# First roots and squares moved to GpSimd, first products issued by operand, 24 filler matmuls: a two-layer MLP kernel on one core

## The chip, the cores and the metric

One Trainium2 chip, one core. The time is device microseconds (us) of one execution. Engines are named as in the profile: PE (TensorE), DVE (VectorE), ACT (ScalarE), POOL (GpSimd), SP (SyncE, which issues most DMAs).

## The reference

x is (2, 2048, 512). Layer 0 is a conditioned RMS norm, a gated MLP and an 8-bit/ternary down projection; layer 1 is an adapter whose weights are themselves made from the condition.

```python
scale = cond @ norm_w.T + 1.0
ms = mean(x * x, axis=-1)
h = x * (scale * rsqrt(ms + 1e-6))
val, gate = split(h @ up_w.T)              # up_w: 4096 x 512
h = val * gelu(gate)
y = act_quant(h) @ weight_quant(down_w).T + x
Wd_b = Wd + 0.1 * (cond @ Wdd.T + bdd)     # Wdd, Wdu: 65536 x 128
Wu_b = Wu + 0.1 * (cond @ Wdu.T + bdu)
out = y + relu(y @ Wd_b.T + bd) @ Wu_b.T + bu
```

## The kernel before, in words

Rows of x are taken in eight blocks of 512 tokens, two blocks (0 and 1, then 2 and 3, and so on) to a stage. In each stage 16 quads (`for n in range(NQ)`) compute the up projection of two blocks with seven products p1 to p7 per quad (a Strassen-like scheme: `product(n, p)`, lines 1351 to 1355), each product of two operands split into a high and a low fp16 part. `t_mov` holds the moving operands made of x, `u_e` and `u_l` the rows of `up_w`. In between run the adapter weights (`adapter_group(g)`, line 1406, 32 x 512 f32 matmuls on the tiles loaded from `Wdd` and `Wdu`), the down projection and, late, the adapter itself.

Every engine has its own program, written out by hand; each runs strictly in its written order, and semaphores (`wait_ge`) tie them together. The change touches the prologue, the first 40 us:

- ACT squares blocks 0 and 1 (`first_squares`, line 972), DVE adds the squares (lines 1791 and 1798), PE multiplies the sums with a tile of ones (`stat(0)`, line 1420, for block 0, `stat1(0)` and `stat1(1)`, line 1429, for block 1), and DVE makes the mean (`mean_square`, line 1822) and ten small chained instructions of inverse square root (`rsqrt(0)`, `rsqrt(1)`, lines 1834 to 1850).
- PE spreads the roots over the partitions (`spread_rs(0)` into `b_ps`, `spread_rs(1)` into `c_ps`, line 1439). DVE then scales x by them: `x_scaled(0, ...)` in two halves for block 0 and `x_scaled(1)`, four instructions, for block 1 (line 1876).
- ACT (`t_high`, line 1058) and DVE (`t_low`, line 1907) split the scaled x into the moving operands B11, B21, B12, B22. PE runs `first_product` for each (lines 1383, 1389, 1393).
- On PE the order around it is: first product of B11, `adapter_group(0)`, `spread_rs(1)`, `adapter_group(1)` and `(2)`, first product of B21, `adapter_group(3)`, `bounds(1, 2)`, `adapter_group(4)`, the products of B12 and B22, `adapter_group(5)` and `(6)`, and then quad 1.
- POOL sets `ones` and `ident` (lines 872 to 875), waits for both roots (`s_rs` 2) and then runs `weight_sums` (lines 898 to 905), sums of rows of `up_w` which ACT and DVE split from quad 1 on. At the end of each stage POOL runs `partition_all_reduce` (lines 916, 927, 934), and in stage 1 also `down_sums` (line 949), elementwise sums.

POOL's program also holds instructions called MODIFY_POOL_CONFIG in the trace and ISA in the instruction order; the build puts one ahead of the first elementwise instruction behind a `partition_all_reduce`, and one ahead of the first `partition_all_reduce` behind an elementwise one.

## Time and profile before

| | us |
|---|---|
| median of 3 runs | 839.31 |
| the three runs | 839.36, 838.85, 839.31 |
| the profiled execution | 840.44 |
| its span, first to last instruction | 838.7 |
| PE busy | 821.2 |
| DVE busy | 664.3 |
| ACT busy | 399.8 |
| POOL busy | 121.3 |

The profiled execution's own time lies 1.7 us over its span (launch and end around it) and 1.1 us over the median of the runs. A timeline row gives the start and the length of an instruction (or of a merged few), and in brackets the idle time of its engine ahead of it and what ended that. The clock column PEclk prints 1.00 in all stretches of this profile.

### The profile page before, as it was taken

To read this page: it belongs to the slowest core of one execution; us is meant where nothing else is said; L and a number is where in the kernel's file an instruction comes from. 1 tells how busy PE (TensorE), PEld (TensorE's weight loads), DVE (VectorE), ACT (ScalarE), POOL (GpSimd) and SP (SyncE) were. 2 spreads that over 40 slices of the span, in tenths; PEclk is the share of its full clock that TensorE was granted. 3 is DMA by queue.
4 is the path that set the end of the run, shared out by engine and by line. 5 is a ranking of instruction groups with operands and counts; after the bars stand their busy time and mean duration, and the time that the engine had idled before them with its cause. 6 is when DMAs were issued, how large, how long until landed. Compare 5 with 4: busy or idle time off the path is not lost.

```text
span 838.7 us, 11856 instructions
## 1 busy us (share of the span) xinstructions
PE 821.2 (98%) x3914; PEld 359.4 (43%) x3914; DVE 664.3 (79%) x968; ACT 399.8 (48%) x653; POOL 121.3 (14%) x91
## 2 busy tenths in 40 slices
PE   5999999999999999999999999999999999999998
PEld 4334444444344334444444444444444444444443
DVE  5998787889878889767787678988986586675986
ACT  5778887776454532227445543326433333324000
POOL 0363332302001153300101011100200000001000
PEclk9999999999999999999999999999999999999999
DMA  9879989666899862377798865337247435435232
GB/s 343 338 257 347 343 289 297 233 217 226 303 347 366 330 218 95 136 271 272 280 326 303 304 223 191 116 95 255 72 137 239 138 95 189 138 95 176 101 125 76
DMA packets 64860, 186.65 MB, mean 223 GB/s; under 512 B 7072, under 2 KB 8352, under 8 KB 64416
## 3 DMA queue, kind: packets, MB, share of 16 engines
q1 hardware_dynamic: 64512, 185.63, 63.5%
q8 instruction: 33, 0.54, 0.3%
q10 hardware_dynamic: 288, 0.26, 0.1%
q14 instruction: 27, 0.22, 0.1%
HBM read 154.41 MB, written 30.41 MB: 220 GB/s over the span
## 4 chain that ended last, share of the span: by engine, by line
PE 85%; DVE 5%; issue 3%; ACT 1%; DVEq 0%; ACTq 0%
PE b_ps L1351 9%; PE b_ps L1355 9%; PE b_ps L1353 9%; PE aux_ps L1406 6%; PE a_ps L1351 6%; PE aux_ps L1464 6%; PE a_ps L1355 6%; PE a_ps L1353 6%; PE c_ps L1351 3%; PE aux_ps L1542 3%; PE e_ps L1351 3%; PE e_ps L1355 3%; PE e_ps L1353 3%; PE c_ps L1353 3%; PE c_ps L1355 3%
## 5 line engine op out<-in xcount | busy, mean ns | idle before, releaser
L1954 DVE SCALAR_TENSOR_TENSOR h_ring<-v_sb,unscale,gelu 128x512 f32<-128x512 f32 x63 | 55.5, 881 | 58.0 <-ACT gelu L1092 31.9
L1351 PE MATMUL b_ps<-t_mov,u_l 128*128 128x512 f16 x252 | 95.5, 379 | 3.8 <-DVE c_ps L1915 3.6
L1355 PE MATMUL b_ps<-t_mov,u_l 128*128 128x512 f16 x252 | 95.5, 379 | 0.0
L1353 PE MATMUL b_ps<-t_mov,u_l 128*128 128x512 f16 x252 | 95.5, 379 | 0.0
L1978 DVE TENSOR_TENSOR hmax<-gelu,hmax 128x512 f32<-128x512 f32 x120 | 88.6, 740 | 7.8 <-ACT gelu L1098 2.9
L1068 ACT ACTIVATE b_ps<-a_ps 128x512 f32<-128x512 f32 x63 | 36.7, 582 | 94.1 <-PE a_ps L1355 93.9
L1102 ACT ACTIVATE gelu<-h_ring 128x512 f32<-128x512 f32 x64 | 40.3, 629 | 67.6 <-DVE h_ring L1954 67.6
L2013 DVE TENSOR_TENSOR h_ring<-h_ring,qscale 128x1024 f16<-128x1024 f32 x48 | 64.7, 1387 | 0.0
L1084 ACT ACTIVATE gelu<-a_ps,unscale 128x512 f32<-128x512 f32 x64 | 43.7, 682 | 43.3 <-DVE hmax L1978 41.1
L916 POOL PARTITION_ALL_REDUCE yscale<-hmax x8 | 17.9, 2266 | 321.0 <-DVE hmax L1978 320.3
L1098 ACT ACTIVATE gelu<-h_ring 128x512 f32<-128x512 f32 x64 | 40.2, 628 | 45.6 <-DVE h_ring L1964 45.3
L1964 DVE SCALAR_TENSOR_TENSOR h_ring<-b_ps,unscale,gelu 128x512 f32<-128x512 f32 x64 | 47.8, 747 | 15.9 <-PE b_ps L1355 15.5
L1092 ACT ACTIVATE gelu<-c_ps,unscale 128x512 f32<-128x512 f32 x64 | 43.9, 686 | 32.9 <-PE c_ps L1355 32.9
L1406 PE MATMUL aux_ps<-w_ring,cond_sb 128*32 128x512 f32 x480 | 58.1, 599 | 0.0
L1075 ACT ACTIVATE p_sb<-e_ps 128x512 f32<-128x512 f32 x63 | 37.5, 595 | 37.5 <-PE e_ps L1355 27.4
L1923 DVE TENSOR_TENSOR v_sb<-b_ps,p_sb 128x512 f32<-128x512 f32 x63 | 43.3, 687 | 11.4 <-PE b_ps L1355 11.2
L1351 PE MATMUL e_ps<-t_mov,u_e 128*128 128x512 f16 x126 | 47.8, 379 | 0.8 <-DVE u_e L1743 0.8
L1351 PE MATMUL b_ps<-t_mov,u_e 128*128 128x512 f16 x126 | 47.8, 379 | 0.8 <-ACT b_ps L1068 0.8
L1351 PE MATMUL a_ps<-t_mov,u_e 128*128 128x512 f16 x126 | 48.0, 381 | 0.0
L1351 PE MATMUL c_ps<-t_mov,u_l 128*128 128x512 f16 x126 | 47.8, 379 | 0.1
L1353 PE MATMUL e_ps<-t_mov,u_e 128*128 128x512 f16 x126 | 47.8, 379 | 0.0
L1355 PE MATMUL e_ps<-t_mov,u_e 128*128 128x512 f16 x126 | 47.8, 379 | 0.0
(264 smaller groups left out, 1701.4 us busy)
## 6 DMA issues: line engine op xcount, KB each, us to landing
w_ring<-in_Wdu SPq DMA_DIRECT2D x64, 512.0 KB, 6.0
w_ring<-in_Wdd SPq DMA_DIRECT2D x56, 512.0 KB, 7.2
u_l<-ul_dram SPq DMA_DIRECT2D x48, 512.0 KB, 4.7
u_e<-ue_dram SPq DMA_DIRECT2D x48, 384.0 KB, 3.2
h_ring<-in_up_w SPq DMA_DIRECT2D x16, 512.0 KB, 6.4
x_sb<-in_x SPq DMA_DIRECT2D x8, 1024.0 KB, 7.9
res<-in_down_w SPq DMA_DIRECT2D x16, 512.0 KB, 7.1
ul_dram<-u_l SPq DMA_DIRECT2D x15, 512.0 KB, 5.6
```

What stands on the lines that cost most here:

```text
L1084: act.activation(gelu1[:, :], a_ps[n % 2][:, :], ACT.Gelu, scale=unscale[:, s // 2, j:j + 1]).then_inc(s_g1, 1)
L1092: act.activation(gelu2[:, :], c_ps[:, :], ACT.Gelu, scale=unscale[:, s // 2, j:j + 1]).then_inc(s_g2, 1)
L1351: pe.matmul(ps[:, :], weight(n, p, 0, k), hi, start=fresh and k == 0, stop=False, skip_group_check=True)
L1353: pe.matmul(ps[:, :], weight(n, p, 0, k), lo, start=False, stop=False, skip_group_check=True)
L1355: mm = pe.matmul(ps[:, :], weight(n, p, 1, k), hi, start=False, stop=k == 1, skip_group_check=True)
L1406: mm = pe.matmul(ps[32 * q:32 * q + 32, :], cond_sb[:, :], w_tile(n)[:, 512 * (q % 2):512 * (q % 2) + 512], start=True, stop=True)
L1464: mm = pe.matmul(ps[:, :], w, q_slot(d, at + c)[:, TB * t:TB * t + TB], start=fresh and c == 0, stop=c == HC - 1, skip_group_check=True)
L1923: dve.tensor_tensor(v_sb[:, :], b_ps[n % 2][:, :], p5_sb[:, :], ALU.add)\
L1954: dve.scalar_tensor_tensor(out=h_slot(n)[:, TB:TS], in0=val[:, :], scalar=unscale[:, s // 2, j:j + 1], in1=gelu2[:, :], op0=ALU.mult, op1= ...
L1964: dve.scalar_tensor_tensor(out=h_slot(n)[:, 0:TB], in0=b_ps[n % 2][:, :], scalar=unscale[:, s // 2, j:j + 1], in1=gelu1[:, :], op0=ALU.mul ...
L1978: dve.tensor_tensor(total, absolute, total, ALU.max).then_inc(done, 1)
L2013: dve.tensor_tensor(q_slot(s, c), h_slot(NP * s + c), qscale[:, :], ALU.mult)\
```

## The change

- POOL sets a third tile, `power` (-0.5), and computes the two inverse roots itself: `first_roots(t)` raises the mean squares to that power with one 128x4 elementwise instruction each. DVE's `rsqrt(0)` and `rsqrt(1)` go; the later `rsqrt` calls stay.
- The squares of block 1 are summed to one tile by DVE (a third addition, `second_sum_squares(2)`), then over the partitions by a `partition_all_reduce` on POOL, between the two `first_roots`. DVE masks the result with `ident` and reduces it. PE's `stat1(0)` and `stat1(1)` go, and so does the wait for them ahead of SP's loads of the tiles 8 to 11 of `Wdd` (the squares now lie elsewhere in `h_ring`).
- PE runs 16 matmuls on the tile of ones (read as fp16, 256 columns, into `a_ps1`, whose contents are not used) ahead of its first work and 8 more behind it.
- PE's two first products (B11) are written out operand by operand: the terms that need only high parts first, those that need low parts behind them.
- ACT makes B21's high part ahead of `row_sums(2)` and waits for `s_rs` 2 ahead of `stage_group(1)`.

```diff
@@ -295,6 +295,7 @@
         ms_half = sb("ms_half", [P, 2 * NT])
+        power = sb("power", [P, NT])
         rs = sb("rs", [P, 2, 2 * NT])
@@ -313,6 +314,10 @@
         aux_ps = [ctx.enter_context(nc.psum_tensor(f"aux_ps{n}", [P, TB], F32)) for n in range(2)]
+        first_squares1 = [h_ring[:, k, TB:TS] for k in range(KD)]
+        first_total = h_ring[:, 2, TB:TS]
+        first_grid = first_total.rearrange("p (t q) -> p t q", t=NT)

@@ -605,8 +610,6 @@
                 if n in EARLY_SLOT:
-                    if n >= 8:
-                        sp.wait_ge(s_stat1, 2)
                     sp.dma_start(w_tile(n), src[n]).then_inc(s_w_early[n], 16)
@@ -871,7 +874,8 @@
             pool.memset(ident[:, :], 1.0).then_inc(s_const, 1)
-            pool.wait_ge(s_const, 2)
+            pool.memset(power[:, :], -0.5).then_inc(s_const, 1)
+            pool.wait_ge(s_const, 3)
             pool.affine_select(out=ident[:, :], in_=ident[:, :], compare_op=ALU.is_equal, fill=0.0,
@@ -918,7 +922,18 @@

-            pool.wait_ge(s_rs, 2)
+            def first_roots(t):
+                pool.wait_ge(s_ms, t + 1)
+                cols = slice(NT * t, NT * t + NT)
+                pool.tensor_tensor(rs[:, 0, cols], ms[:, cols], power[:, :], ALU.pow)\
+                    .then_inc(s_rs, 1)
+            first_roots(0)
+            pool.wait_ge(s_sq1, 3)
+            pool.partition_all_reduce(first_total, first_squares1[0], P, AR.add)\
+                .then_inc(s_stat1, 1)
+            first_roots(1)
             for j in SUM_ORDER:
@@ -969,7 +984,8 @@
                     act.wait_ge(s_x0[KD * t + k], 16)
-                    act.activation(h_ring[:, KD * t + k, 0:TB], x_sb[:, t, k, :], ACT.Square)\
+                    act.activation(h_ring[:, k, TB * t:TB * t + TB], x_sb[:, t, k, :],
+                                   ACT.Square)\
                         .then_inc(s_sq, 1)
@@ -1193,9 +1209,10 @@
             u_high(0, 2)
+            t_high(0, B21)
             row_sums(2)
             stage_group(0)
-            t_high(0, B21)
+            act.wait_ge(s_rs, 2)
             stage_group(1)
@@ -1356,12 +1373,7 @@

-            def first_product(ps, first_half, val, m):
-                if first_half and val:
-                    pe.wait_ge(s_first_hi, 1)
-                else:
-                    pe.wait_ge(s_uhi, part_count(0, 0 if first_half else 2))
+            def first_operands(first_half, val, m):

@@ -1373,13 +1385,17 @@

-                if m == B11:
-                    pe.wait_ge(s_first_row, 1)
+                return rows, split
+            def first_product(ps, first_half, val, m):
+                rows, split = first_operands(first_half, val, m)
+                if first_half and val:
+                    pe.wait_ge(s_first_hi, 1)
                 else:
-                    pe.wait_ge(s_thi, split_count(0, m))
+                    pe.wait_ge(s_uhi, part_count(0, 0 if first_half else 2))
+                pe.wait_ge(s_thi, split_count(0, m))
                 for k in range(2):
-                    if m == B11 and k == 1:
-                        pe.wait_ge(s_thi, 1)
                     pe.matmul(ps[:, :], rows(0, k), split(0, k), start=first_half and k == 0,
@@ -1420,16 +1436,6 @@
                 mm.then_inc(s_stat if i else s_aux, 1)
-            def stat1(part):
-                pe.wait_ge(s_sq1, part + 1)
-                row = KD + 2 * part
-                for t in range(NT):
-                    mm = pe.matmul(e_ps[:, NT * part + t:NT * part + t + 1],
-                                   h_ring[:, row, P * t:P * t + P], ones[:, 0:1],
-                                   start=True, stop=True)
-                mm.then_inc(s_stat1, 1)

@@ -1568,21 +1574,56 @@

+            half_ones = ones[:, :].bitcast(F16)
+            def keep_busy(count):
+                pe.wait_ge(s_const, 1)
+                for _ in range(count):
+                    pe.matmul(a_ps[1][:, 0:2 * P], half_ones[:, 0:P], half_ones[:, :],
+                              start=True, stop=True)
+            keep_busy(16)
             pe.wait_ge(s_small, 32)
...
             mm.then_inc(s_aux, 1)
-            pe.wait_ge(s_const, 1)
+            keep_busy(8)
             stat(0)
-            stat1(0)
             first_bounds()
-            pe.wait_ge(s_const, 3)
+            pe.wait_ge(s_const, 4)
             spread_rs(0)
-            stat1(1)
-            first_product(a_ps[0], True, False, B11).then_inc(s_p[1], 1)
-            first_product(b_ps[0], True, True, B11).then_inc(s_p[5], 1)
+            gate, val = first_operands(True, False, B11), first_operands(True, True, B11)
+            pe.wait_ge(s_uhi, part_count(0, 0))
+            pe.wait_ge(s_first_row, 1)
+            for k in range(2):
+                if k:
+                    pe.wait_ge(s_thi, 1)
+                pe.matmul(a_ps[0][:, :], gate[0](0, k), gate[1](0, k), start=(k == 0),
+                          stop=False, skip_group_check=True)
+            pe.wait_ge(s_first_hi, 1)
+            for k in range(2):
+                pe.matmul(b_ps[0][:, :], val[0](0, k), val[1](0, k), start=(k == 0),
+                          stop=False, skip_group_check=True)
+            pe.wait_ge(s_ulo, part_count(0, 0))
+            for k in range(2):
+                pe.matmul(a_ps[0][:, :], gate[0](1, k), gate[1](0, k), start=False,
+                          stop=False, skip_group_check=True)
+            pe.wait_ge(s_tlo, split_count(0, B11))
+            for k in range(2):
+                mm = pe.matmul(a_ps[0][:, :], gate[0](0, k), gate[1](1, k), start=False,
+                               stop=(k == 1), skip_group_check=True)
+            mm.then_inc(s_p[1], 1)
+            for k in range(2):
+                pe.matmul(b_ps[0][:, :], val[0](0, k), val[1](1, k), start=False,
+                          stop=False, skip_group_check=True)
+            pe.wait_ge(s_first_lo, 1)
+            for k in range(2):
+                mm = pe.matmul(b_ps[0][:, :], val[0](1, k), val[1](0, k), start=False,
+                               stop=(k == 1), skip_group_check=True)
+            mm.then_inc(s_p[5], 1)
             adapter_group(0)
@@ -1590,7 +1631,6 @@
             adapter_group(3)
-            pe.wait_ge(s_ms, 2)
             bounds(1, 2, e_ps).then_inc(s_total, 1)
@@ -1793,20 +1833,23 @@

-                row = KD + 2 * part
-                dve.wait_ge(s_sq, row + 2)
-                dve.tensor_tensor(h_ring[:, row, 0:TB], h_ring[:, row, 0:TB],
-                                  h_ring[:, row + 1, 0:TB], ALU.add).then_inc(s_sq1, 1)
+                if part < 2:
+                    dve.wait_ge(s_sq, KD + 2 * part + 2)
+                    a, b = first_squares1[2 * part:2 * part + 2]
+                else:
+                    dve.wait_ge(s_sq1, 2)
+                    a, b = first_squares1[0], first_squares1[2]
+                dve.tensor_tensor(a, a, b, ALU.add).then_inc(s_sq1, 1)

...

-                    dve.wait_ge(s_stat1, 2)
+                    dve.wait_ge(s_stat1, 1)
+                    dve.wait_ge(s_const, 4)
                     total = ms_half[:, col:col + NT]
-                    link(dve.tensor_reduce(
-                        total, e_ps[:, 0:2 * NT].rearrange("p (k t) -> p t k", k=2),
-                        AX_X, ALU.add))
+                    link(dve.tensor_tensor(first_grid, first_grid, diagonal, ALU.mult))
+                    link(dve.tensor_reduce(total, first_grid, AX_X, ALU.add))
                 elif i >= 4:
@@ -1822,15 +1865,11 @@

-            def rsqrt(i, count=1):
-                s, t = divmod(i, 2)
-                cols = slice(NT * t, NT * t + NT * count)
-                dve.wait_ge(s_ms, i + count)
-                if i == 0:
-                    dve.wait_ge(s_table, 1)
-                a, half, t = ms[:, cols], ms_half[:, cols], rs_t[:, cols]
-                y = rs[:, s % 2, cols]
+            def rsqrt(i):
+                dve.wait_ge(s_ms, i + 2)
+                a, half, t = ms[:, :], ms_half[:, :], rs_t[:, :]
+                y = rs[:, (i // 2) % 2, :]
                 link(dve.tensor_scalar(half, a, -0.5, None, ALU.mult))
@@ -2170,20 +2209,20 @@
             mean_square(0)
-            rsqrt(0)
             aux_ready(dve, "total", 0)
...
             u_low(0, 0)
+            second_sum_squares(2)
             t_low(0, B11)
...
             second_scales()
-            mean_square(1)
-            rsqrt(1)
             x_scaled(0, (2, 3))
             u_low(0, 2)
+            dve.wait_ge(s_table, 1)
+            mean_square(1)
             t_low(0, B21)
```

The order of POOL's instructions from its first tile on, before:

```order
L872 MEMSET ones 128x128
L873 MEMSET ident 128x128
L875 ISA
L875 AFFINE_SELECT ident<-ident 128x128 [waits s_const]
L898 TENSOR_TENSOR yscale<-h_ring 128x256 [waits s_u1,s_rs]
L901 TENSOR_TENSOR yscale<-yscale,h_ring 128x256 [waits s_us]
```

and now (the ISA at L934 with operands is the `partition_all_reduce`):

```order
L875 MEMSET ones 128x128
L876 MEMSET ident 128x128
L877 MEMSET power 128x4
L879 ISA
L879 AFFINE_SELECT ident<-ident 128x128 [waits s_const]
L929 TENSOR_TENSOR rs<-ms,power 128x4 [waits s_ms]
L934 ISA
L934 ISA h_ring<-h_ring 128x512 [waits s_sq1]
L929 ISA
L929 TENSOR_TENSOR rs<-ms,power 128x4 [waits s_ms]
L902 TENSOR_TENSOR yscale<-h_ring 128x256 [waits s_u1]
```

Between the affine select and the weight sums stand now two roots, one `partition_all_reduce` and two more configuration instructions, one ahead of the reduction and one ahead of the second root.

PE's order from the last matmul of the first products on, as it is now (before, the same instructions follow in the same order; the adapter group is L1406 there and the spread L1439):

```order
L1624 MATMUL b_ps<-t_mov,v_sb 128x512
L1422 MATMUL aux_ps<-w_ring,cond_sb 32x512 [waits s_w0,s_ms]
L1422 MATMUL aux_ps<-w_ring,cond_sb 32x512
L1422 MATMUL aux_ps<-w_ring,cond_sb 32x512 [waits s_w1]
L1422 MATMUL aux_ps<-w_ring,cond_sb 32x512
L1445 MATMUL c_ps<-ident,rs 128x128 [waits s_rs]
L1445 MATMUL c_ps<-ident,rs 128x128 x3
L1422 MATMUL aux_ps<-w_ring,cond_sb 32x512 [waits s_w2,s_top]
```

The spread of block 1's roots (into `c_ps`) keeps its place; all of PE's later work stands behind its wait for `s_rs`.

## Rows read from the trace of the kernel before

**Rows 1.** The page, part 1: busy us, share of the span, instructions of each engine.
```profile
PE 821.2 (98%) x3914; PEld 359.4 (43%) x3914; DVE 664.3 (79%) x968; ACT 399.8 (48%) x653; POOL 121.3 (14%) x91
```
**Rows 2.** Waits of PE, whole span: us in total, times, longest us.
```profile
PE aux_ps L1574 <- DMA cond_sb<-in_cond: 5.3, 1, 5.3
PE b_ps L1351 <- DVE c_ps L1915: 3.6, 6, 1.6
PE aux_ps L1420 <- DVE h_ring L1791: 2.5, 1, 2.5
PE e_ps L1351 <- DVE u_e L1743: 0.8, 1, 0.8
PE b_ps L1351 <- ACT b_ps L1068: 0.8, 1, 0.8
```
**Rows 3.** Busy us by stretch, 26 to 56 us; then clock, DMA share, GB/s.
```profile
26.00:36.00 10.00, 9.99 (x58) 3.83 (x62) 9.82 (x17) 6.97 (x10) 4.32 (x5) 1.00 1.03 408
...
46.00:56.00 10.00, 9.38 (x47) 3.73 (x46) 10.00 (x12) 6.99 (x12) 9.84 (x10) 1.00 0.97 342
```
**Rows 4.** Timeline of PE: start us, us, engine, line, operands.
```profile
13.90 1.09 PE L1439 MATMUL b_ps<-ident,rs 128*128 128x128 f32 x4
...
17.47 0.59 PE L1383 MATMUL a_ps<-t_mov,u_e 128*128 128x512 f16 x1
...
19.99 0.47 PE L1383 MATMUL b_ps<-t_mov,v_sb 128*128 128x512 f16 x1
20.29 0.38 PE L1389 MATMUL b_ps<-t_mov,v_sb 128*128 128x512 f16 x1
20.51 0.38 PE L1383 MATMUL b_ps<-t_mov,v_sb 128*128 128x512 f16 x1
...
22.46 0.65 PE L1439 MATMUL c_ps<-ident,rs 128*128 128x128 f32 x4
```
**Rows 5.** Timeline of DVE, prologue.
```profile
11.52 0.16 DVE L1822 TENSOR_SCALAR ms<-aux_ps 128x4 f32<-128x4 f32 x1 [0.69 <-PE aux_ps L1420]
...
13.51 0.16 DVE L1850 SCALAR_TENSOR_TENSOR rs<-rs_t,rs 128x4 f32<-128x4 f32 x1
...
15.61 1.40 DVE L1876 SCALAR_TENSOR_TENSOR x_sb<-b_ps,cs_x,x_sb 128x512 f32<-128x512 f32 x2
...
21.94 0.16 DVE L1850 SCALAR_TENSOR_TENSOR rs<-rs_t,rs 128x4 f32<-128x4 f32 x1
...
25.88 2.71 DVE L1876 SCALAR_TENSOR_TENSOR x_sb<-c_ps,cs_x,x_sb 128x512 f32<-128x512 f32 x4
```
**Rows 6.** Timeline of POOL, prologue and stage 1.
```profile
11.54 0.28 POOL L875 TENSOR_SCALAR_AFFINE_SELECT ident<-ident 128x128 f32<-128x128 f32 x1 [10.41 <-issue]
22.19 0.73 POOL L898 TENSOR_TENSOR yscale<-h_ring 128x256 f32<-128x256 f32 x1 [10.37 <-DVE rs L1850]
...
291.45 4.14 POOL L927 PARTITION_ALL_REDUCE res<-res  x1 [28.94 <-DVE res L1899]
305.85 3.82 POOL L949 TENSOR_TENSOR w_ring<-wq 128x2048 fp8e4<-128x2048 fp8e4 x1 [10.27 <-issue]
...
324.01 3.25 POOL L934 PARTITION_ALL_REDUCE res<-res  x1 [5.86 <-issue]
335.14 3.82 POOL L949 TENSOR_TENSOR w_ring<-wq 128x2048 fp8e4<-128x2048 fp8e4 x1 [7.89 <-issue]
```
**Rows 7.** The configuration instructions of line L949: ns min/median/max, first and last start.
```profile
L949 POOLq MODIFY_POOL_CONFIG  x4: 88/93/98, 295.5 to 327.2; - x4
```
**Rows 8.** Stretches as in rows 3, around POOL's gaps and in the prologue.
```profile
295.60:305.80 10.20, 10.20 (x56) 4.08 (x55) 8.01 (x13) 4.64 (x8) 0.00 (x0) 1.00 0.61 212
318.20:324.00 5.80, 5.80 (x29) 2.61 (x27) 5.32 (x17) 2.55 (x4) 0.00 (x0) 1.00 0.00 0
12.00:22.00 10.00, 9.25 (x42) 5.83 (x42) 8.46 (x35) 6.04 (x11) 0.00 (x0) 1.00 1.03 413
```
**Rows 9.** Timeline of ACT, its first use of a weight sum.
```profile
37.06 0.71 ACT L1022 ACTIVATE u_e<-yscale,um_mul 128x512 f16<-128x512 f32 x1
```

More of the change, by code:

```diff
@@ L1850, in rsqrt @@
                 dve.scalar_tensor_tensor(out=y, in0=t, scalar=1.5 * 1.5, in1=y,
-                                         op0=ALU.add, op1=ALU.mult).then_inc(s_rs, count)
+                                         op0=ALU.add, op1=ALU.mult).then_inc(s_rs, 2)
             def spread_roots(i):
@@ L2318, in _ @@
                 if j == ROOTS and s + 1 < NSB:
-                    rsqrt(2 * s + 2, 2)
+                    rsqrt(2 * s + 2)
                     if s:
```

## The prediction

> **What bounds the kernel now.** I read the page first, then the waits of PE, then the stretches and timelines of the first 60 us, POOL's timeline last. PE is busy 821.2 of 838.7 us [rows 1], so the kernel is PE's work plus 17.5 us in which PE stands. The waits show where [rows 2]: 5.3 us until the condition has landed, 2.5 us for the sum of squares of block 0, and then small ones: six waits for DVE's `c_ps` (3.6 us in all) and 0.8 us each for `u_e` and `b_ps`. Without the first two, 9.7 us of standing are left in the whole rest of the run. The stretches show the second bound: from 26 to 36 us DVE is busy 9.82 of 10 us, from 46 to 56 us all 10.00 [rows 3]. So from the moment DVE starts `x_scaled(1)` at 25.88 us [rows 5] until about 55 us DVE and PE are both nearly full, and whatever delays that start, or PE's place beside it, has nothing to hide behind. What the change adds has to be looked for on the path to that point, which is: mean of block 1, root, spread, `x_scaled(1)`.
>
> **Parts off that path.** The 24 filler matmuls have 256 columns. A 512-column matmul comes every 0.43 us at 17.47 us and every 0.22 us at 20.29 us [rows 4], while the profile grants the full clock throughout; those two rates are what 1.2 and 2.4 GHz give. So a filler costs at most 0.22 us: 16 of them 3.4 us from about 1.0 us on, inside the 5.3 us wait; 8 of them at most 1.7 us, inside the 2.5 us wait [rows 2]. Cost nothing; without that cover it would be up to 5 us. What they may bring is the higher rate earlier: the six matmuls from 17.47 to 19.99 us would take 1.3 instead of 2.5 us. Issuing the first products by operand and dropping the two groups of `stat1` also bring PE to its next task earlier. That task is `spread_rs(1)` behind one adapter group, and it waits for the root; all of this gain goes into that wait. The same goes for block 0: the root leaves DVE at 13.67 us [rows 5] and PE starts the spread at 13.90 us [rows 4]; now POOL can start it when its affine select is over, 11.54 + 0.28 = 11.8 us [rows 6], so x of block 0 is scaled some 1.3 us earlier, and DVE reaches its wait for block 1 earlier. Nothing of it survives if block 1's root is late. SP's four loads of `Wdd` tiles lose a wait that had been satisfied when the queue came to them, since they stand behind a store that starts at the same time: nothing. ACT's new wait for `s_rs` 2 holds back `stage_group(1)` and, through it, adapter group 3 on PE; both belong behind `spread_rs(1)` in any case: nothing beyond the delay itself. POOL's weight sums start after the second root instead of at 22.19 us; the first is read by ACT at 37.06 us [rows 9], 14.9 us later, and that reader moves with the delay: nothing.
>
> **The path itself: POOL.** The order shows two new configuration instructions, one ahead of the reduction and one ahead of the second root. What they cost is in POOL's timeline [rows 6]: the first elementwise instruction stands 10.41 us behind the memsets and waits for nothing shown. In stage 1 an elementwise sum stands 10.27 us behind a reduction and another, of which the order shows no wait at all, 7.89 us; the configuration instruction itself takes 0.1 us and is issued at 295.5 us, as the reduction ends [rows 7]. In the other direction a reduction stands 5.86 us behind a sum (a second such gap is 5.93 us). The gaps come with little and with much DMA traffic: 10.27 us at a DMA share of 0.61, 5.86 us at 0.00; in the prologue the share is 1.03 [rows 8]. These are switches of code, and none of them is hidden for an in-order engine.
>
> Step by step, in us from the span's start:
> - POOL free at 11.9 (11.8 and one more small memset); the mean of block 0 is there at 11.68 [rows 5]. A root of 128x4 elements on POOL has no row. It lies between 0.1 (memsets of one column) and 0.73 (a sum of 128x256 [rows 6]); I take 0.2, as it is near the small end in elements. End 12.1.
> - Switch to the reduction: 5.9, from the only rows of that direction; the upper bound is the 10.41 of the start, which had the DMA traffic. End 18.0. The third sum of squares on DVE is ready by then: it is 0.7 us of work behind `x_scaled(0)`, which before ended at 17.0 [rows 5].
> - Reduction of 128x512: 4.14 or 3.25 [rows 6]; I take 4.1, the row that also sums squares. End 22.1. DVE's mask, reduce and mean behind it (0.7 + 0.7 + 0.2, the 0.7 from the scaling instructions of the same 128x512 [rows 5]) end near 23.7, in the shadow of the next step.
> - Switch back: 10.3, between ends of 7.9 and 10.4; two of three rows say 10.3, and they are the ones with more DMA traffic. End 32.4, root 0.2, signal 0.1: PE starts `spread_rs(1)` at 32.7. Before, at 22.46 [rows 4].
>
> That is 10.2 us later for PE. By then PE has stood for about 12 us and I expect it to begin at the lower rate, as it did at 17.47 us: spread 1.1 us like block 0's [rows 4], and 1.3 us lost until the rate rises. Against that stand the small waits it will now find satisfied, 0.8 + 0.8 for `u_e` and `b_ps` [rows 2]. PE: 10.2 + 1.3 - 1.6 = 9.9. DVE starts `x_scaled(1)` at 32.7 + 1.1 + 0.1 = 33.9 instead of 25.9: 8.0 later. The two lanes then wait for each other (DVE's `c_ps` needs p6, PE's p7 needs `c_ps`), so the end moves by something between 8.0 and 9.9; I take 9.0. The stages behind follow with the same work and waits.
>
> The Trainium skill bears on the second switch ("GPSIMD Engine Reference", section 2.1): the first call into freshly loaded code pays about 6 us (5.95) that no profile row shows. The trace agrees for the switch to the reduction (5.86), not for the way back (7.89 and 10.27).
>
> **Sum.** 839.3 + 9.0 = 848.3 for the median; for a profiled execution 840.4 + 9.0 = 849.4, span near 847.7. The forecast's own ends: low, with the reduction at 3.25, the way back at 7.9, the roots at 0.1 and the end moving with DVE alone, the spread starts at 12.0 + 5.9 + 3.2 + 7.9 + 0.2 = 29.2, DVE moves by 4.5: 843.8. High, with the first switch at 10.3 under full DMA traffic and roots of 0.7: spread at 37.6, PE moves by 15.1 + 1.3 - 1.6 = 14.8: 854.1.
>
> **Rivals.**
> - *The switches are not paid here* (faster). Place: the two configuration instructions on POOL. If code of both kinds stays usable, the reduction starts with the third sum of squares, near 16.9 (x of block 0 scaled at 15.7, a 128x256 split and the sum behind it), and ends at 21.0; DVE's mean follows at 22.6, the root at 22.9, and DVE, which has one split of 1.4 us left to do ahead of it, starts `x_scaled(1)` at about 24.2, 1.7 us earlier: 837.6. The sign turns where the way back costs some 3 us, the reduction ending at 22.1: the root would then be there at 25.3, the start at 26.1. Against it: both kinds of code had been loaded before 318 us, and every change of kind still shows its gap [rows 6]. Chance 0.08.
> - *Both switches cost 6 us.* Spread at 12.1 + 5.9 + 4.1 + 5.9 + 0.3 = 28.3; PE moves by 5.8 + 1.3 - 1.6 = 5.5: 844.8. Against it is only the direction of the two gaps of 7.89 and 10.27 us. The skill's figure for the first call (same page and section) gives the same case. Chance 0.10.
> - *The delay is absorbed.* PE stands for 10.2 us more at `spread_rs(1)`, and at most 9.7 us of standing lie elsewhere; if DVE's lane had slack everywhere and all of them closed, 0.5 us would be left: 839.8, no change. Against it: DVE is full until 56 us [rows 3]. Chance 0.04.
> - The forecast, with its own ends, has the rest, 0.78.
>
> **How the numbers follow.** 0.2% is 1.7 us, about what a measurement of this kernel can tell from no change. The forecast and the second rival are slower: 0.88; the third is within: 0.04; the first is faster: 0.08. The range from 843.0 to 854.5 holds the forecast's ends and the second rival and leaves out 0.12.
>
> **What would show it.** Right: on POOL the first root near 12 us, the reduction at 18 us or later, a gap of 8 to 10 us with no releaser between it and the second root; PE with one long wait for that root ahead of `spread_rs(1)`; `x_scaled(1)` on DVE 5 to 12 us later; the stretches from 60 us on unchanged but shifted. Wrong: a second root within 3 us of the mean of block 1, or PE's waits between 35 and 56 us grown instead of shrunk.

## The result: 854.4 us against 839.4 us, and the profile after

The change took 854.38 us (median of 5, 852.26 to 855.34) against 839.36 us for the kernel before in the same job (838.85 to 840.02): the ratio is 1.0179, interval 1.0167 to 1.0190, so 15.0 us slower. In a second job it took 852.54 us against 839.5, ratio 1.0148 (1.0129 to 1.0167), 13.1 us slower. The profiled execution took 853.41 us with a span of 851.7, 13.0 more than the span before; the explanation is made against these 13.0.

The page of the changed kernel, busy time first and then two of its 40-slice rows:

```profile
PE 826.3 (97%) x3922; PEld 360.5 (42%) x3922; DVE 662.1 (78%) x950; ACT 398.9 (47%) x653; POOL 126.3 (15%) x95
...
PE   7499999999999999999999999999999999999998
...
PEclk9699999999999999999999999999999999999999
```

PE works 5.1 us more than in [rows 1] (24 fillers and matmuls at the lower rate, less 16 of `stat1`), so it stands 25.4 instead of 17.5 us. The second slice, about 21 to 43 us, is the hole: PE busy four tenths, granted clock six tenths. PE's waits in the changed kernel (us in total, times, longest), against [rows 2]:

```profile
PE c_ps L1445 <- POOL rs L929: 12.5, 1, 12.5
PE b_ps L1368 <- DVE c_ps L1954: 2.7, 6, 0.8
PE a_ps L1604 <- ACT t_mov L1070: 2.5, 1, 2.5
PE b_ps L1368 <- ACT b_ps L1084: 1.4, 1, 1.4
PE aux_ps L1590 <- DMA cond_sb<-in_cond: 1.2, 1, 1.2
```

The two waits of the prologue, 5.3 and 2.5 us, have given way to fillers, shorter waits (1.2 us here for the condition) and a new one of 2.5 us for ACT's first split. All of that lies ahead of one wait of 12.5 us for the second root, which was not in [rows 2] at all. POOL's timeline in the changed kernel shows what it waits for, against [rows 6] (start us, us, operation; in brackets the idle time before and its releaser):

```profile
10.68 0.28 POOL L879 TENSOR_SCALAR_AFFINE_SELECT ident<-ident 128x128 f32<-128x128 f32 x1 [9.51 <-issue]
11.19 1.06 POOL L929 TENSOR_TENSOR rs<-ms,power 128x4 f32<-128x4 f32 x1 [0.22 <-DVE ms L1865]
21.65 3.25 POOL L934 PARTITION_ALL_REDUCE h_ring<-h_ring  x1 [9.40 <-issue]
32.89 1.05 POOL L929 TENSOR_TENSOR rs<-ms,power 128x4 f32<-128x4 f32 x1 [7.99 <-issue]
33.93 0.71 POOL L902 TENSOR_TENSOR yscale<-h_ring 128x256 f32<-128x256 f32 x1
```

Its configuration instructions at these two lines (ns min/median/max, first and last start in us), and DVE's timeline behind them, where the mean is ready long before POOL can use it:

```profile
L934 POOLq MODIFY_POOL_CONFIG  x2: 11/11/11, 12.5 to 12.5; - x2
L929 POOLq MODIFY_POOL_CONFIG  x2: 98/98/98, 24.8 to 24.9; - x2
```
```profile
26.43 0.17 DVE L1865 TENSOR_SCALAR ms<-ms_half 128x4 f32<-128x4 f32 x1
...
35.14 2.73 DVE L1915 SCALAR_TENSOR_TENSOR x_sb<-c_ps,cs_x,x_sb 128x512 f32<-128x512 f32 x4 [7.41 <-PE c_ps L1445]
```

Each configuration instruction is issued within 0.3 us of its predecessor's end (12.25 and 24.90 us) and lasts at most 0.1 us; the next operation of the other kind comes 9.40 and 7.99 us behind that end, with nothing named but "issue". The mean is there at 26.60, 6.3 us before the root starts. `x_scaled(1)` starts at 35.14 instead of 25.88 [rows 5]. The third sum of squares ended at 16.17 us, so the reduction, too, had its input 5.5 us before it started.

PE's timeline behind the wait, changed kernel:

```profile
33.99 1.11 PE L1445 MATMUL c_ps<-ident,rs 128*128 128x128 f32 x4 [12.46 <-POOL rs L929]
35.03 1.94 PE L1422 MATMUL aux_ps<-w_ring,cond_sb 128*32 128x512 f32 x8
36.74 1.93 PE L1422 MATMUL aux_ps<-h_ring,cond_sb 128*32 128x512 f32 x8
38.61 0.61 PE L1399 MATMUL a_ps<-t_mov,u_l 128*128 128x512 f16 x1
...
40.66 0.38 PE L1399 MATMUL b_ps<-t_mov,u_l 128*128 128x512 f16 x1
...
44.36 0.39 PE L1399 MATMUL c_ps<-t_mov,u_e 128*128 128x512 f16 x1
...
55.84 0.38 PE L1368 MATMUL b_ps<-t_mov,u_e 128*128 128x512 f16 x1 [1.35 <-ACT b_ps L1084]
```

In the kernel before, the second product of B21 (into `b_ps`), the first of B12 (into `c_ps`) and PE's last wait of the first 60 us:

```profile
26.45 0.38 PE L1383 MATMUL b_ps<-t_mov,u_l 128*128 128x512 f16 x1
...
30.15 0.39 PE L1383 MATMUL c_ps<-t_mov,u_e 128*128 128x512 f16 x1
...
55.86 0.38 PE L1351 MATMUL b_ps<-t_mov,u_l 128*128 128x512 f16 x1 [0.62 <-DVE c_ps L1915]
```

The `c_ps` product at 44.36 was at 30.15 before: PE is 11.5 us late at the spread (33.99 against 22.46 [rows 4]) and 14.2 us late here. The stretches show why (PE, PEld, DVE, ACT, POOL busy us, granted clock, DMA share, GB/s), and then the one from 47 to 107 us before, to set beside the last:

```profile
24.90:32.90 8.00, 0.00 (x0) 0.00 (x0) 2.67 (x4) 0.00 (x0) 0.01 (x1) 0.60 0.97 388
...
32.00:42.00 10.00, 8.01 (x32) 2.58 (x32) 4.41 (x6) 3.66 (x5) 6.93 (x8) 0.59 0.36 136
42.00:52.00 10.00, 10.00 (x63) 3.69 (x63) 8.85 (x15) 5.75 (x10) 1.80 (x2) 1.00 0.28 83
60.00:120.00 60.00, 59.79 (x308) 25.71 (x301) 50.41 (x91) 49.31 (x90) 26.20 (x29) 1.00 0.96 322
```
```profile
47.00:107.00 60.00, 59.38 (x305) 25.79 (x302) 50.40 (x91) 49.34 (x90) 26.22 (x29) 1.00 0.95 322
```

PE does nothing for 8 us, the granted clock is 0.60 then and 0.59 in the next ten, and the two adapter groups take 1.9 us each instead of 1.07 and 1.04. From the spread to the second product of B21 PE needs 6.67 us (33.99 to 40.66), before 3.99 (22.46 to 26.45): 2.7 us lost. From 42 us on the clock is full. Shorter waits then give back about 1.1 us: the product that waited 0.62 us for `c_ps` at 55.86 before waits 0.21 us here, at 68.97, 13.1 us late. From there on the stretches hold the same work (DVE 50.41 and 50.40 us, ACT 49.31 and 49.34), and the 13.0 us of the span come from the first 69 us.

### The profile page after: what moved, and what is told of

Read it like the earlier page. It is cut to its first block, busy times and chain, and to the rows that moved or that the text cites. A ratio compares the mean times of both kernels' runs of the same rounds, so it can differ in the third digit from the quotient of the medians.

```text
span 851.7 us, 11858 instructions
## 1 busy us (share of the span) xinstructions
PE 826.3 (97%) x3922; PEld 360.5 (42%) x3922; DVE 662.1 (78%) x950; ACT 398.9 (47%) x653; POOL 126.3 (15%) x95
## 4 chain that ended last, share of the span: by engine, by line
PE 81%; DVE 6%; issue 3%; ACT 1%; DMA 1%; DVEq 0%; ACTq 0%
PE b_ps L1368 8%; PE b_ps L1370 8%; PE b_ps L1372 8%; PE aux_ps L1422 6%; PE a_ps L1368 6%; PE a_ps L1372 6%; PE a_ps L1370 6%; PE aux_ps L1470 4%; PE aux_ps L1548 3%; PE c_ps L1368 3%; PE e_ps L1370 3%; PE e_ps L1368 3%; PE e_ps L1372 3%; PE c_ps L1370 3%; PE c_ps L1372 3%
## 5 line engine op out<-in xcount | busy, mean ns | idle before, releaser
L2003 DVE SCALAR_TENSOR_TENSOR h_ring<-b_ps,unscale,gelu 128x512 f32<-128x512 f32 x64 | 47.8, 748 | 15.5 <-PE b_ps L1372 15.1
L1368 PE MATMUL b_ps<-t_mov,u_e 128*128 128x512 f16 x126 | 47.8, 379 | 1.4 <-ACT b_ps L1084 1.4
L1368 PE MATMUL c_ps<-t_mov,u_l 128*128 128x512 f16 x126 | 47.8, 379 | 0.1
L1368 PE MATMUL e_ps<-t_mov,u_e 128*128 128x512 f16 x126 | 47.8, 379 | 0.0
L1370 PE MATMUL e_ps<-t_mov,u_e 128*128 128x512 f16 x126 | 47.8, 379 | 0.0
L1372 PE MATMUL e_ps<-t_mov,u_e 128*128 128x512 f16 x126 | 47.8, 379 | 0.0
```

The source lines that it names most:

```text
L1368: pe.matmul(ps[:, :], weight(n, p, 0, k), hi, start=fresh and k == 0, stop=False, skip_group_check=True)
L1370: pe.matmul(ps[:, :], weight(n, p, 0, k), lo, start=False, stop=False, skip_group_check=True)
L1372: mm = pe.matmul(ps[:, :], weight(n, p, 1, k), hi, start=False, stop=k == 1, skip_group_check=True)
L2003: dve.scalar_tensor_tensor(out=h_slot(n)[:, 0:TB], in0=b_ps[n % 2][:, :], scalar=unscale[:, s // 2, j:j + 1], in1=gelu1[:, :], op0=ALU.mul ...
```

## The experiments

Times are medians, and each ratio is against the kernel before in the same job. The change itself was timed in two jobs (854.38 and 852.54 us), and neither job holds the first four or the last four experiments; these are set beside it by ratio and by the spans and rows of single profiled executions. The change's own two spans are 851.7 and 850.8 us, so differences of a span under 1 us say nothing.

### Reduction back on PE, the rest of the change kept

```diff
-            pool.wait_ge(s_sq1, 3)
-            pool.partition_all_reduce(first_total, first_squares1[0], P, AR.add)\
-                .then_inc(s_stat1, 1)
             first_roots(1)
...
             stat(0)
+            stat1(0)
             first_bounds()
...
             spread_rs(0)
+            stat1(1)
```

with the two-group sum on DVE again, and `mean_square(1)` ahead of `x_scaled(0, (2, 3))`.

> The change without the reduction on POOL: block 1's squares are summed by PE with the tile of ones as before, both roots stay on POOL, and the fillers, the operand order of the first products and ACT's wait stay. Theory A (the two code switches around the reduction are the cost): no switch ahead of the second root, x_scaled(1) on DVE starts near 23 us instead of 35.1, and the time is 2 to 3 us under the kernel before, 836 to 838 us. Theory B (fillers, ACT's wait, operand order or the slow root on POOL, 1.05 us, carry a part): the time stays at least 3 us over the kernel before.

838.80 us against 839.23, ratio 0.9996 (0.9987 to 1.0006), span 836.1. The 836 to 838 us expected were missed. One of 12 executions stood out at 4929 us; no profile shows that one. Everything slow about the change has gone, with roots, fillers, operand order and ACT's wait still in it. POOL's timeline here:

```profile
11.00 1.05 POOL L929 TENSOR_TENSOR rs<-ms,power 128x4 f32<-128x4 f32 x1
19.05 1.01 POOL L929 TENSOR_TENSOR rs<-ms,power 128x4 f32<-128x4 f32 x1 [6.99 <-DVE ms L1874]
```

No switch, so the root waits for its mean alone. `x_scaled(1)` starts at 22.90 us, 3.0 earlier than before, and yet no time is won: `c_ps` of B12 starts at 29.45 instead of 30.15, since PE's own work fills the stretch, and then a wait of PE that was 0.8 us is longer:

```profile
40.93 0.38 PE L1365 MATMUL b_ps<-t_mov,u_e 128*128 128x512 f16 x1 [1.35 <-ACT b_ps L1081]
```

### PE kept busy up to the second root

```diff
             adapter_group(0)
+            keep_busy(110)
             spread_rs(1)
```

> The change with 110 more fillers (256 columns) between adapter group 0 and spread_rs(1), so that PE is busy through its 12.5 us wait for the root. Theory A with a clock part: in the changed kernel PE resumes at half rate and loses 2.7 us (6.67 us from the spread to the end of B21's first product instead of 3.99); with the gap filled this comes back, 12.3 us over the kernel before instead of 15.0, near 851.7. Without a clock part the time stays at 854.

851.48 us, ratio 1.0143 (1.0129 to 1.0157), span 850.1. POOL came to the root at 33.97 us and PE to the spread at 35.08, 1.1 us later than in the change, behind gaps of 8.95 and 9.31 us; with PE at work, 9.07 us passed from the spread to `c_ps` of B12 instead of 10.37. So 1.3 of the 2.7 us came back. The fillers ended 2.3 us before the root was there, and the granted clock from 34 to 41 us was 0.76, against 0.56 in the change: not a clean removal of the low rate. It bounds its share from below. That the median hit the expected 851.7 us is in part luck: the expectation counted down from 854.38, and against the change's other median, 852.54, only 1.1 us came back.

### Fillers taken away

```diff
-            keep_busy(16)
             pe.wait_ge(s_small, 32)
...
-            keep_busy(8)
+            pe.wait_ge(s_const, 1)
             stat(0)
```

> The change without its 24 fillers. Theory A: they lie in PE's first waits, and what they bring ends in the wait for the root: 854 us, within 1.5 us of the change. Rival: the fillers themselves cost time, and it falls by 2 us or more.

852.67 us, ratio 1.0157 (1.0142 to 1.0171), span 851.6, 0.1 from the change's. PE's wait for the root was 13.6 us. The fillers neither cost nor bring anything that these runs can tell.

### The second root on DVE: only the way back leaves the path

```diff
                 .then_inc(s_stat1, 1)
-            first_roots(1)
...
             mean_square(1)
+            rsqrt(1, 1)
             t_low(0, B21)
```

> The change with block 1's root on DVE (ten small instructions, 2.1 us) right behind its mean; the reduction stays on POOL, and the switch back then stands ahead of the weight sums alone. Theory A: the spread starts near 28.8 us instead of 34.0, 9 to 10.5 us over the kernel before, 848 to 850 us. Rival (the second switch is hidden or cheap, the reduction and the first switch are all of it): within 2 us of the change.

847.65 us, ratio 1.0102 (1.0086 to 1.0119), span 846.1: 5.6 us less than the change's. PE's timeline here:

```profile
29.13 1.11 PE L1444 MATMUL c_ps<-ident,rs 128*128 128x128 f32 x4 [7.54 <-DVE rs L1890]
```

It is still 6.7 us behind 22.46 [rows 4]. The reduction started at 22.13 behind a gap of 9.97 us, so this run leaves the first switch and the reduction on the path, and its remaining 7.4 us of span are their price. The spread comes 4.9 us earlier than in the change, and not the 7.99 + 1.05 us of the way back and its root: the mask, the reduce and the mean on DVE (1.7 us), which the gap had hidden, now stand on the path, DVE's root, ten instructions from 27.12 us on, takes 2.0 us, and the reduction started 0.5 us later here. The time is just under the 848 to 850 us expected.

### The switches off the path: small probes behind weight sums of quads 2, 7 and 15

```diff
+                pool.partition_all_reduce(scratch[:, 0:2], scratch[:, 4:6], P, AR.add)\
+                    .then_inc(s_cm, 1)
+                pool.wait_ge(s_cm, 2 * n + 2)
+                pool.tensor_tensor(scratch[:, 2:4], scratch[:, 0:2], scratch[:, 0:2],
+                                   ALU.add).then_inc(s_cm, 1)
...
                 weight_sums(j)
+                if j in PROBES:
+                    probe(PROBES.index(j))
```

in the kernel before.

> The kernel before with three pairs added on POOL, behind the weight sums of quads 2, 7 and 15: a reduction of 128x2 and an elementwise sum of 128x2 right behind it, with no other engine to wait for. The gap ahead of each is then a switch alone. The first pair stands near 30 us (DMA share 1.03, reduction code not used before), the second near 85 us (share 0.98, used before), the third near 170 us (share about 0.5). Theory A1 (a first switch of 9.4 us in the changed kernel because the DMA queues are full): 9 us at the first and the second pair, 6 at the third. Theory A2 (because that code had not been used before): 9 us at the first pair only, 6 at both others. The switch back costs 7.8 to 10.3 in all three. The time grows where a switch holds up weight sums that ACT waits for; it is not what this run is for.

One execution: 840.08 us, span 838.4 against 838.7. POOL's timeline:

```profile
34.89 0.65 POOL L927 PARTITION_ALL_REDUCE small<-small  x1 [6.24 <-issue]
42.41 0.49 POOL L930 TENSOR_TENSOR small<-small 128x2 f32<-128x2 f32 x1 [6.87 <-issue]
...
95.97 0.43 POOL L927 PARTITION_ALL_REDUCE small<-small  x1 [10.80 <-issue]
104.57 0.18 POOL L930 TENSOR_TENSOR small<-small 128x2 f32<-128x2 f32 x1 [8.17 <-DVE u_e L1757]
...
178.23 0.41 POOL L927 PARTITION_ALL_REDUCE small<-small  x1 [8.99 <-issue]
185.37 0.38 POOL L930 TENSOR_TENSOR small<-small 128x2 f32<-128x2 f32 x1 [6.74 <-issue]
```

The profile puts the gap ahead of 104.57 us down to DVE's `u_e`, but in the program that sum waits for the reduction alone. Three things follow. Three pairs of switches, 47.8 us of POOL's time, did not lengthen the span of this one execution: a switch costs only what waits for POOL. The gap comes at every change of kind in both directions, and the first use in the program had the shortest of the three (6.24), so it is not the price of a first use. Both theories in the expectation asked for 9 us at the first pair, and both fall. The DMA shares of the six gaps are, in order, 1.03, 0.48, 1.01, 1.01, 0.84, 0.30: with 0.48 and less 6.7 to 6.9 us, with more 6.2 to 10.8. Traffic may stretch it, but 6.24 at 1.03 stands against a rule.

### Fillers alone, in the kernel before

```diff
+            keep_busy(16)
             pe.wait_ge(s_small, 32)
...
-            pe.wait_ge(s_const, 1)
+            keep_busy(8)
             stat(0)
```

> The kernel before with the 24 fillers alone. If fillers in PE's first waits cost nothing and bring the higher rate for a while, DVE's lane (full from 26 to 56 us) keeps the end where it is: within 0.2% of the kernel before. A gain of 1 us or more would say that PE's lane sets the end of the prologue; a loss of 1 us or more would say that the fillers themselves cost.

839.73 us, ratio 0.9998 (0.9986 to 1.0010). PE's timeline:

```profile
5.74 1.05 PE L1584 MATMUL aux_ps<-cond_sb,stage 128*128 128x2 f32 x8 [1.40 <-DMA cond_sb<-in_cond]
...
9.17 1.86 PE L1420 MATMUL aux_ps<-ones,h_ring 128*128 128x1 f32 x8 [1.24 <-DVE h_ring L1801]
```

The first group came at the higher rate (before it took 1.87 us), but from 9 to 20 us the granted clock was 0.50: the rate won in the wait was lost again before the products.

### The change once more

The same kernel, in the probes' job.

> The change itself once more, on the chip of this job, to be set beside the run without fillers: 1.0157 to 1.0179 of the kernel before. The wait of PE for the second root is 12 to 13 us long again.

852.54 us, as above; span 850.8. The ratio, 1.0148, is a little under the range expected and the wait a little over. Gaps of 8.79 and 8.74 us, PE's wait 13.1 us, the spread at 34.49. The split between the two gaps varies (9.40 and 7.99 in the first trace), their sum hardly (17.4 and 17.5).

### More fillers, without the reduction

Against the first experiment's kernel:

```diff
-            keep_busy(8)
+            keep_busy(20)
             stat(0)
+            keep_busy(3)
             stat1(0)
+            keep_busy(3)
             first_bounds()
...
             spread_rs(0)
+            keep_busy(6)
             stat1(1)
```

> The version without the reduction on POOL, with 20 fillers in place of 8 behind the scale, and 3, 3 and 6 more between the small groups that follow. In the run without the reduction PE ran the scale group in 1.05 us at the higher rate and fell back at about 9 us, while the groups up to 16 us took 1.7 to 1.9 each. If fillers between them hold the rate, the groups take about 1 us each, spread_rs(1) comes some 2 us earlier and the time falls to about 837. If they don't hold it, they only add their own 0.2 us each, and the time is 1 to 2 us over the run without the reduction.

839.46 us, ratio 0.9999 (0.9985 to 1.0014), span 837.2. PE's timeline:

```profile
7.28 3.71 PE L1589 MATMUL a_ps<-ones 128*128 128x256 f16 x20
10.82 0.95 PE L1433 MATMUL aux_ps<-ones,h_ring 128*128 128x1 f32 x8
```

The group of `stat(0)` now takes 0.95 instead of 1.73 us, but the fillers hold it back from 8.59 to 10.82 us, and `spread_rs(1)` comes at 22.26 instead of 21.31. The groups took about 1 us each, as expected, but `spread_rs(1)` did not come earlier and the time did not fall to 837. The higher rate can be had in the prologue; bought with work ahead of the path, it brings nothing.

### One more pair of switches on the path

```diff
             first_roots(0)
+            pool.wait_ge(s_cm, 1)
+            pool.partition_all_reduce(small[:, 4:6], power[:, 0:2], P, AR.add)\
+                .then_inc(s_cm, 1)
+            pool.wait_ge(s_cm, 2)
+            pool.tensor_tensor(small[:, 6:8], small[:, 4:6], small[:, 4:6], ALU.add)\
+                .then_inc(s_cm, 1)
             pool.wait_ge(s_sq1, 3)
```

> The change with one more pair of switches on the same path: between the first root and the reduction POOL runs a reduction of 128x2 and an elementwise sum of 128x2, whose results nobody reads. Theory A (the time is the chain of switches ahead of the second root): the pair costs 6 to 10 us out, 7 to 8 back and about 1 us of work, 14 to 19 us, and PE's wait for the second root grows by the same: 867 to 873 us. Rival (something else bounds the prologue in the changed kernel, and the switches hide behind it): less than half of that.

867.35 us, ratio 1.0330 (1.0313 to 1.0347), span 866.7: 15.0 above the change's. POOL's timeline and PE's longest wait:

```profile
21.68 0.41 POOL L934 PARTITION_ALL_REDUCE small<-power  x1 [9.61 <-issue]
32.24 0.18 POOL L937 TENSOR_TENSOR small<-small 128x2 f32<-128x2 f32 x1 [10.16 <-issue]
38.35 3.25 POOL L940 PARTITION_ALL_REDUCE h_ring<-h_ring  x1 [5.92 <-issue]
48.57 1.05 POOL L929 TENSOR_TENSOR rs<-ms,power 128x4 f32<-128x4 f32 x1 [6.98 <-issue]
```
```profile
PE c_ps L1451 <- POOL rs L929: 28.3, 1, 28.3
```

The two tiny operations take 0.6 us together; the wait grew by 15.8 and the span by 15.0. So the added pair costs its switches, not its operations. Its own gaps are 9.61 and 10.16 us, at DMA shares of 1.02 and 1.03; the two that stood there already, now without traffic (shares of 0.04 and 0.00), are 5.92 and 6.98 instead of 9.40 and 7.99, together 4.5 us shorter, and that is why the wait grew by less than 20 us.

### Both roots on DVE, only the reduction on POOL

```diff
-            first_roots(0)
             pool.wait_ge(s_sq1, 3)
...
             mean_square(0)
+            dve.wait_ge(s_table, 1)
+            rsqrt(0, 1)
```

against the kernel with the second root on DVE.

> The change with both roots on DVE; of POOL's part only the reduction is left, and its first switch starts right behind the affine select. Against the version with the second root alone on DVE the reduction starts about 1.3 us earlier (no wait for the mean, no root of 1.05 us ahead of the switch), so the time is about 1 us less, 846 to 847 us; still 7 us over the kernel before, since one switch of 9 us and 3.25 us of reduction stand ahead of the second root.

847.17 us, ratio 1.0092 (1.0074 to 1.0109), span 845.4. The reduction started at 20.98 us behind a gap of 9.48: the switch cannot begin before the affine select is over (11.50 us), so taking the first root away wins 1.2 us at the spread (27.97 against 29.13) and, as far as two spans can tell, 0.7 at the end. The third sum is ready at 16.95 us in this trace: even so arranged, the first switch alone keeps the reduction 4.0 us behind it.

### Operand order alone, and roots alone, in the kernel before

```diff
-            first_product(a_ps[0], True, False, B11).then_inc(s_p[1], 1)
-            first_product(b_ps[0], True, True, B11).then_inc(s_p[5], 1)
+            gate, val = first_operands(True, False, B11), first_operands(True, True, B11)
...
+            pe.wait_ge(s_ulo, part_count(0, 0))
+            for k in range(2):
+                pe.matmul(a_ps[0][:, :], gate[0](1, k), gate[1](0, k), start=False,
+                          stop=False, skip_group_check=True)
```

> The kernel before with the operand order of the first products alone. PE has no wait inside these products before (its rows stand back to back from 17.47 us), so nothing is gained: within 0.2% of the kernel before.

839.38 us, ratio 1.0000 (0.9988 to 1.0012). For the roots:

```diff
+            for t in range(2):
+                pool.wait_ge(s_ms, t + 1)
+                cols = slice(NT * t, NT * t + NT)
+                pool.tensor_tensor(rs[:, 0, cols], ms[:, cols], power[:, :], ALU.pow)\
+                    .then_inc(s_rs, 1)
...
             mean_square(0)
-            rsqrt(0)
...
             mean_square(1)
-            rsqrt(1)
```

> The kernel before with its two first roots on POOL and nothing else. DVE is freed of 20 small instructions (4 us) in a stretch where it is full, and x_scaled(1) starts 1.5 to 3 us earlier. If that reaches the end, 837 to 838 us. In the version without the reduction, x_scaled(1) started 3.0 us earlier and the time fell by 0.4 us only, PE's B12 product being 0.7 us earlier; if that holds here too, 838.5 to 839.5 us.

838.98 us, ratio 0.9994 (0.9985 to 1.0003), span 838.3. Roots at 10.95 and 19.34 us, the second done 2.0 us ahead of the spread, which PE reaches only at 22.33 in its own order. Both edits: no difference.

## Why the prediction was right, and where it fell short

Direction and mechanism held: two switches of code stand ahead of the second root, PE waits for it once (12.5 us; forecast about 12), `x_scaled(1)` moves by 9.3 us (5 to 12 were asked for), the stages behind are shifted whole. Without the switches the time is that of before; with one fewer on the path it lies between; with one more pair it grows by 15.0. The size was too small: forecast +9.0, profiled +13.0, medians +15.0 and +13.1. The median of 854.38 is 0.1 us inside the range, and that is luck: it lies above the high end that the forecast worked out for itself, 854.1. That sum has an error, too: with a first switch of 10.3 and two roots of 0.7 the spread comes at 32.7 + 4.4 + 0.5 + 0.5 = 38.1, not 37.6, and the high end is 854.6, past the range's own limit of 854.5.

- **POOL free at 11.9, root 0.2.** The affine select ended at 10.96, earlier, but a root takes 1.05 us, above the 0.73 that was set as its upper bound. "Near the small end in elements" was the wrong reason: operations were taken to cost by their elements, and the power of 128x4 costs more than the sum of 128x256 at 22.19 us. Its end, 12.25, is 0.15 late; at the second root the miss is 0.85.
- **Switch to the reduction, 5.9.** This was the largest miss: 9.40. Both rows of that direction were from stage 1; one had a DMA share of 0.00. The forecast saw the share of 1.03 in the prologue and put 10.3 only in the range.
- **Reduction, 4.1.** Measured 3.25, the row of L934 in [rows 6]: 0.85 too long. The two rows to choose from are the same call in the kernel, an addition over the partitions, so that summing squares was no reason for the longer one; why they differ is not known.
- **Switch back, 10.3.** Measured 7.99: 2.3 too long. The two misses nearly cancel (17.4 us of gaps against 16.2); root and reduction cancel too. The spread came at 33.99 against 32.7, 1.3 late.
- **PE's lower rate, 1.3.** Measured 2.7. It began at the lower rate as forecast, but stayed there for 6 us, through the spread, two adapter groups and a product, where the example that the forecast took, six matmuls from 17.47 to 19.99 us, had only 2.5 us at that rate and lost 1.3. The loss was counted over the example's work and not over the work behind this wait.
- **Waits found satisfied, -1.6.** The 0.8 us for `u_e` went and the six for `c_ps` fell by 0.9, but the one for ACT's `b_ps` grew from 0.8 to 1.4: -1.1.
- **The end between the lanes, 9.0.** It moved with PE: 11.5 + 2.7 - 1.1 = 13.1. DVE was 9.3 late at `x_scaled(1)`, but 13.3 late at `c_ps` of block 1 (57.34 against 44.08), and busy 4.41 of 10 us from 32 to 42 (the rows are below). Once DVE waited for PE, by way of ACT, its lane was no longer full, and the mean of two lanes had nothing to stand for. The later lane decides. Of the 4.0 us that the forecast fell short, 1.3 are the spread, 1.4 the rate, 0.5 the waits and 0.9 this mean (4.1 by the rounded parts).

How PE's delay reaches DVE, from ACT's and DVE's timelines in the changed kernel:

```profile
38.74 0.60 ACT L1129 ACTIVATE h_ring<-aux_ps 128x512 f32<-128x512 f32 x1 [1.05 <-PE aux_ps L1422]
39.24 1.99 ACT L1074 ACTIVATE t_mov<-x_sb 128x1024 f16<-128x1024 f32 x2
```
```profile
40.32 2.90 DVE L1946 TENSOR_TENSOR t_mov<-x_sb,t_mov 128x1024 f16<-128x1024 f32 x2 [2.45 <-ACT t_mov L1074]
```

ACT waits for PE's slow adapter group before it splits the scaled x, and DVE stands 2.45 us for that split; before, DVE's split at 28.52 us followed `x_scaled(1)` without a wait.

Parts costed at nothing showed no cost: fillers (839.73 against 839.5), operand order (839.38 against 839.44), roots (838.98 against 839.44); with all of these and ACT's wait in it, but no reduction on POOL, 838.80 against 839.23.

**The rivals.** "Not paid" falls by the gaps themselves. "Absorbed" falls by the stretch from 60 us on, whose standing and work are those of before. "Both 6 us" named 844.8: the gaps were 9.40 and 7.99. Here the Trainium skill ("GPSIMD Engine Reference", section 2.1) says that a first call into freshly loaded code costs about 6 us that no row shows. The rows agree that none shows it, and that some gaps are near that figure (5.92 and 6.24 us); they differ in size, since most gaps are longer, up to 10.8 us. The measurement decides. That it is paid at each change of kind, also for code that ran before, fits the rule if the code is loaded anew each time, which no row here shows.

**Open.** What sets a gap between 5.7 and 10.8 us is not settled. It is no first use, and the short ones are mostly in stretches with little DMA traffic, but 6.24 us came at a share of 1.03. In stage 1 the gaps repeat in all 14 traces: 5.7 to 6.2 us to each of the two reductions, 8.4 to 10.3 and 7.7 to 8.6 us on the two ways back (DMA shares before: 0.00 and 0.38, 0.61 and 0.40). Place and traffic change together there, so these rows do not part them. Nor is it settled why the medians of the change lie 2 us apart in two jobs while those of the kernel before lie within 0.3.

## What to carry to other kernels

Before a job is moved to an engine, look in its timeline for what stands between operations of different kinds: an idle time before "issue", with nothing that releases it, is a price the new place will pay again (here at each change of kind, in both directions), and it counts whenever someone waits for that engine (here 15.0 us for one more pair on the path, nothing for three off it). When an engine is made to stand, add what it does at a lower clock afterwards, counted over the work that really follows. And where two full lanes wait for each other, take the later one, not a mean.

## What the runs showed of the hardware beyond that

- A power of 128x4 elements takes 1.05 us on POOL, where sums of 128x256 take 0.71 to 1.79; a partition reduction takes 3.25 us for 128x512 and 0.41 to 0.65 us for 128x2. The gap, not the operation, is what a small reduction costs.
- The change and the first experiment begin with the same instructions, and yet the first group of small matmuls took 1.86 us in the one and 1.05 us in the other, each behind 16 fillers of 0.22 us, the spacing of 1.2 GHz for 256 columns. So which rate the first group gets is not fixed by the instructions ahead of it; what does is open.
- The profile's granted clock reads 1.00 from 0 to 5 us, where these fillers run at 0.22 us each, the spacing of the lower rate; a 512-column matmul every 0.43 us in [rows 4] has the same under a printed 1.00. In the prologue the durations tell the rate, the printed clock does not until it has changed once: from 9 to 12 us it reads 0.50 in the run without the reduction on POOL, where the groups take 1.73 us.
